# Expert stage of a cross-attention and mixture-of-experts kernel: raw w1 in two buffers, the high part of the gelu output by a second gelu, gathers ahead of both scatters, unused units not taken

## What is computed

```
x = x + attention(layernorm(x), ctx)            # 16 heads, 154 keys
n = layernorm(x)
for each expert e of 8:                         # two best of softmax(n @ router_w.T)
    h = gelu(n @ w1[e].T)                       # 256 -> 1024, exact gelu
    out = out + weight_e[:, None] * (h @ w2[e].T)   # 1024 -> 256
x = x + out
```

## Time and profile before

| | |
|---|---|
| median of 3 runs | 501.27 us |
| profiled execution | 504.29 us, its span 502.1 us |
| mean granted TensorE clock | 0.938 |
| PE busy | 430.2 us, 86% of the span |
| DVE busy | 364.7 us |
| POOL busy | 263.7 us |
| ACT busy | 222.6 us |
| expert stage (first matmul of `up(0)` to the end) | 237.44 to 502.1 us |

### The profile page before, as it was taken

How to read it: one execution, slowest core, us unless ns; L and a number is a source line. 1 busy time by engine, 2 the same in 40 slices (tenths; PEclk the granted TensorE clock), 3 DMA queues, 4 the chain that set the end, 5 groups by cost and what they waited for, 6 DMA issues and landing times.

```text
span 502.1 us, 11066 instructions
## 1 busy us (share of the span) xinstructions
PE 430.2 (86%) x3429; PEld 378.6 (75%) x3430; DVE 364.7 (73%) x789; ACT 222.6 (44%) x433; POOL 263.7 (53%) x308
## 2 busy tenths in 40 slices
PE   7678999999999998317489999999998699999960
PEld 3577888888888886213389989889997698989950
DVE  2678999999999996596576776765578848775520
ACT  1556667677666775130334424422355444423210
POOL 2678877777787776103304444445434444444452
PEclk9899999999999999657969999999999999999985
DMA  8401112111112111501452542722246734323232
GB/s 236 163 1 44 65 64 76 52 62 53 58 57 84 52 64 33 185 6 42 163 204 44 172 81 44 210 44 44 42 107 171 206 97 110 49 43 54 33 55 33
DMA packets 24769, 42.72 MB, mean 85 GB/s; under 512 B 6048, under 2 KB 19232, under 8 KB 22688
## 3 DMA queue, kind: packets, MB, share of 16 engines
q1 hardware_dynamic: 13664, 28.68, 16.8%
q0 software_dynamic: 7584, 10.80, 12.7%
q10 hardware_dynamic: 3488, 2.83, 1.8%
HBM read 26.54 MB, written 9.45 MB: 72 GB/s over the span
## 4 chain that ended last, share of the span: by engine, by line
PE 59%; DMA 13%; DVE 11%; issue 8%; POOL 5%; ACT 2%; ACTq 1%; DVEq 1%; POOLq 0%
PE ps_s L1245 12%; PE ps_s L1091 10%; PE ps_t L1262 10%; DMA result<-big,rowtok 6%; PE ps_t L1106 6%; PE ps_t L1265 5%; DMA big<-rows,gtok 4%; PE ps_a L1124 3%; PE ps_c L1141 3%; PE ps_a L1047 2%; DMA XS<-in_x 2%; PE ps_a L1119 2%; PE ps_c L1228 2%; PE ps_c L1153 1%; PE ps_c L1147 1%
## 5 line engine op out<-in xcount | busy, mean ns | idle before, releaser
L477 POOL DMA_INDIRECT result<-big,rowtok x38 | 65.3, 1717 | 123.8 <-DVE big L1018 59.7
L1245 PE MATMUL ps_s<-xgT,KB 128*128 128x256 f32 x912 | 113.1, 284 | 12.4 <-DVE KB L933 9.4
L1245 PEld LDWEIGHTS ps_s<-xgT,KB 128*128 128x128 f32 x912 | 110.7, 192 | 14.4 <-DVE KB L933 9.7
L1091 PE MATMUL ps_s<-KB 128*128 (+1 forms) x384 | 72.3, 325 | 9.4 <-DVE V_all L733 3.2
L618 ACT ACTIVATE big<-ps_s 128x512 f32<-128x512 f32 x76 | 44.8, 596 | 74.6 <-PE ps_s L1245 71.3
L446 POOL DMA_INDIRECT big<-rows,gtok x44 | 48.2, 1095 | 52.1 <-DVE gtok L949 24.0
L1091 PEld LDWEIGHTS ps_s<-KB 128*128 128x128 f32 x384 | 57.2, 194 | 14.3 <-issue 7.6
L626 ACT ACTIVATE big<-ps_t,wrow 128x256 f32<-128x256 f32 x38 | 18.0, 474 | 97.0 <-PE ps_t L1265 92.4
L1262 PE MATMUL ps_t<-KB,HTb 128*128 x160 | 57.8, 401 | 0.0
L553 ACT ACTIVATE PT<-ps_t 128x512 f32<-128x512 f32 x80 | 47.5, 599 | 21.5 <-PE ps_t L1106 19.7
L383 POOL TENSOR_TENSOR half<-big 128x256 f32<-128x256 f32 x64 | 47.4, 740 | 16.4 <-ACT big L545 16.1
(11 more groups left out here) (159 smaller groups left out, 779.2 us busy)
## 6 DMA issues: line engine op xcount, KB each, us to landing
big<-in_wexp SPq DMA_DIRECT2D x16, 1024.0 KB
V_cur<-V_all SPq DMA_DIRECT2D x16, 384.0 KB, 2.6
result<-x SPq DMA_DIRECT2D x16, 128.0 KB, 1.7
rows<-xn SPq DMA_DIRECT2D x16, 128.0 KB, 2.1
XS<-in_x ACTq DMA_DIRECT2D x1, 1536.0 KB, 11.4
big<-rows,gtok POOLq DMA_INDIRECT x44
result<-big,rowtok POOLq DMA_INDIRECT x38
big<-in_ctxT SPq DMA_DIRECT2D x1, 308.0 KB, 3.6
```

Source lines behind the costliest of these rows:

```text
L477: pool.indirect_dma_start(out, bass.IndirectOffsetOnAxis(rowtok[:, u, h:h + 1], 0), ys[:, 2 * (u % 2) + h, :], None, compute_op=ALU.add).t ...
L1091: last = mm(ps_s[q % 2][:, j, 0:2 * KEYS].rearrange("p (h k) -> p h k", h=2), a[:, u, g, :], rhs, start=k == 0, stop=k == 2)
L1245: last = mm(ps_s[j // 4][:, j // 2 % 2, (j % 2) * PAIR:(j % 2 + 1) * PAIR], w1[:, w, k, j * P:(j + 1) * P], xgT[:, u % 2, a, k, :], start= ...
```

## The change

- Raw w1 gets two buffers, in space that the attention stage no longer uses (V_all, V_cur and PT are put in one tile VP). SP loads w1[0], w2[0], w1[1] before the first expert is used, and later w1[e+1] right behind w2[e].
- The high part of the gelu output is written by ACT with a second gelu of the same PSUM block (fp32r output), ahead of the plain one. DVE's rounding copy L989 goes; only the subtraction stays (`turn` becomes `low_part`). ACT waits for `down(s-2)` before the gelus of s, where DVE did.
- At the start of the stage DVE's order becomes `take_rows(0)`, `take_rows(1)`, `split_w1(1)`, `low_part(0)`, `split_w2(0)`.
- POOL issues both gathers of unit s+3 ahead of both scatters of s.
- Gathers, `take_rows` and row transposes from unit 16 on are under the condition that their unit is used.

```diff
-        V_all = sb("V_all", [P, B, VW])
-        V_cur = sb("V_cur", [P, 2, VW])
+        VP = sb("VP", [P, (B + 2) * VW + 5 * 4 * P])
+        V_all = VP[:, 0:B * VW].rearrange("p (b v) -> p b v", b=B)
+        V_cur = VP[:, B * VW:(B + 2) * VW].rearrange("p (u v) -> p u v", u=2)
+        PT = VP[:, (B + 2) * VW:].rearrange("p (k a n) -> p k a n", k=5, a=4)
+        wraw1 = VP[:, 0:2 * W1].rearrange("p (e w) -> p e w", e=2)
...
             sp.wait_ge(fold_made, 5 * TILES)
+            sp.wait_ge(pv_psum, TILES)
+            sp.dma_start(wraw1[:, 0, :], wexp[0, :, 0:W1]).then_inc(w1_loaded, 16)
             for e in range(E):
...
                 if e:
-                    sp.wait_ge(w1_lo, NP1 * e)
-                sp.dma_start(wraw1, wexp[e, :, 0:W1]).then_inc(w1_loaded, 16)
-                if e:
                     sp.wait_ge(w2_lo, e)
                 sp.dma_start(wraw2, wexp[e, :, W1:WB]).then_inc(w2_loaded, 16)
+                if e + 1 < E:
+                    sp.wait_ge(w1_loaded, 16 * (e + 1))
+                    if e:
+                        sp.wait_ge(w1_lo, NP1 * e)
+                    sp.dma_start(wraw1[:, (e + 1) % 2, :], wexp[e + 1, :, 0:W1]).then_inc(w1_loaded, 16)
...
                 if has(3):
-                    left_by(s + 1)
+                    with if_used(pool, s + 3):
+                        left_by(s + 1)
+                        for h in range(2):
+                            gather((u + 3) % 4, h)
                 for h in range(2):
-                    if has(3):
-                        gather((u + 3) % 4, h)
                     wait_alone(ys_made, 2 * s + h + 1)
...
-            def gelu(s):
+            def gelu(s, u):
+
+                if not isinstance(s, int) or s >= 2:
+                    act.wait_ge(down_psum, 2 * (s - 1))
                 for b in range(4):
                     act.wait_ge(up_psum, 4 * s + b + 1)
                     if not isinstance(s, int) or s >= 1:
                         act.wait_ge(hidT_lo, 4 * s + b - 3)
+                    act.activation(hidT[u % 2][:, 0, 2 * b:2 * b + 2, :],
+                                   ps_s[b // 2][:, b % 2, :].rearrange("p (j n) -> p j n", j=2), ACT.Gelu)
                     act.activation(hid[:, b, :], ps_s[b // 2][:, b % 2, :], ACT.Gelu).then_inc(hid_made, 1)
...
-            def turn(s, u):
-
-                if not isinstance(s, int) or s >= 2:
-                    dve.wait_ge(down_psum, 2 * (s - 1))
+            def low_part(s, u):
+
                 for b in range(4):
                     js = slice(2 * b, 2 * b + 2)
-                    src = hid[:, b, :].rearrange("p (j n) -> p j n", j=2)
                     dve.wait_ge(hid_made, 4 * s + b + 1)
-                    dve.tensor_copy(hidT[u % 2][:, 0, js, :], src).then_inc(hidT_hi, 1)
-                    dve.wait_ge(hidT_hi, 4 * s + b + 1)
-                    dve.tensor_tensor(hidT[u % 2][:, 1, js, :], src, hidT[u % 2][:, 0, js, :].bitcast(fp32),
-                                      ALU.subtract).then_inc(hidT_lo, 1)
+                    dve.tensor_tensor(hidT[u % 2][:, 1, js, :], hid[:, b, :].rearrange("p (j n) -> p j n", j=2),
+                                      hidT[u % 2][:, 0, js, :].bitcast(fp32), ALU.subtract).then_inc(hidT_lo, 1)
             take_rows(0, 0, True)
-            take_rows(1, 1, True)
-            split_w2(0, 0)
             read_used(dve)
             to_split = dve.value_load(table(t_split, 0), min_val=0, max_val=E * E - 1)
-            turn(0, 0)
+            take_rows(1, 1, True)
             with dve.If(to_split > 0):
                 split_w1(to_split % E)
+            low_part(0, 0)
+            split_w2(0, 0)
...
                 if has(2):
-                    take_rows(s + 2, (u + 2) % 4, has(4))
+                    with if_used(dve, s + 2):
+                        take_rows(s + 2, (u + 2) % 4, has(4))
...
                 if has(2):
-                    row_transposes(s + 2, (u + 2) % 4)
+                    with if_used(pe, s + 2):
+                        row_transposes(s + 2, (u + 2) % 4)
                 down(s, u, e0)
```

More of the change, by code:

```diff
@@ L95, in xattn_moe_kernel @@
         KTr = KB[:, o3:o3 + 2 * GROUPS * B * KEYS].rearrange("p (s g n) -> p s g n", s=2, g=GROUPS)
-        wraw1, wraw2 = big[:, 0:W1], big[:, W1:WB]
+        wraw2 = big[:, W1:WB]
         pr = sb("pr", [P, 2, HEADS, 32])
-        PT = sb("PT", [P, 5, 4, P])
         half = sb("half", [P, 4, 64])
@@ L218, in xattn_moe_kernel @@
             ("xgT_psum", "xgT_made", "gtok_made", "wr1", "wrow_made"))
-        up_psum, hid_made, hidT_hi, hidT_lo, xgT_hi = (sem(n) for n in
-            ("up_psum", "hid_made", "hidT_hi", "hidT_lo", "xgT_hi"))
+        up_psum, hid_made, hidT_lo, xgT_hi = (sem(n) for n in
+            ("up_psum", "hid_made", "hidT_lo", "xgT_hi"))
         down_psum, low_made, ys_made, added = sem("down_psum"), sem("low_made"), sem("ys_made"), sem("added")
@@ L603, in split_w1 @@
                 for cols in PARTS1:
-                    act.activation(ws1[:, 0, cols], wraw1[:, cols], ACT.Copy).then_inc(w1_hi, 1)
+                    src = wraw1[:, e % 2, cols] if isinstance(e, int) else wraw1[:, bass.ds(e % 2, 1), cols].squeeze(1)
+                    act.activation(ws1[:, 0, cols], src, ACT.Copy).then_inc(w1_hi, 1)
             def split_w2(e, par):
@@ L635, in _ @@
             to_split = act.value_load(table(t_split, 0), min_val=0, max_val=E * E - 1)
-            gelu(0)
+            gelu(0, 0)
             with act.If(to_split > 0):
@@ L646, in pair @@
                     with if_used(act, s + 1):
-                        gelu(s + 1)
+                        gelu(s + 1, (u + 1) % 4)
                     with act.If(to_split % E > 0):
@@ L932, in split_w1 @@
                     dve.wait_ge(w1_hi, NP1 * e + n + 1)
-                    dve.tensor_tensor(ws1[:, 1, cols], wraw1[:, cols], ws1[:, 0, cols].bitcast(fp32),
+                    src = wraw1[:, e % 2, cols] if isinstance(e, int) else wraw1[:, bass.ds(e % 2, 1), cols].squeeze(1)
+                    dve.tensor_tensor(ws1[:, 1, cols], src, ws1[:, 0, cols].bitcast(fp32),
                                       ALU.subtract).then_inc(w1_lo, 1)
@@ L1008, in pair @@
                     with if_used(dve, s + 1):
-                        turn(s + 1, (u + 1) % 4)
+                        low_part(s + 1, (u + 1) % 4)
                     with dve.If(to_split % E > 0):
```

## The result

The kernel before took 502.02 us in the comparison (median of 4 runs, 500.98 to 503.67), the changed one 497.3 (494.24 to 503.44): ratio .987 [.983, .991]. It is faster, by about 6.5 us (1.3%) and not by 13.2, and lies outside the range of 484.5 to 493.5. Ratios leave out executions that fell in a slower state (here the one of 503.44 us); medians and ranges are of all executions. The profiled execution of that comparison was that longest of its four.

The account below looks back on a forecast made before the run. The prediction took PE as the bound in the middle of the stage. Start +0.9, middle -11.5 and end -2.6 summed to -13.2 us: span 488.9 from 502.1, or 488.1 us against the median of 501.27, range 484.5 to 493.5.

Parts of the forecast that it names:

- Start: Stage's start through `up(2)`: `up(1)` comes 6.3 us earlier, yet `up(2)` ends at 274.1 against 273.24, 0.9 us later.
- `up(2)` waits for these rows and starts at 266.5: Start: `up(2)` is held until `take_rows(2)` is done, so it starts only 1.1 us earlier than before.
- has 7.9 us to spare: Start: a short stop ahead of `up(1)` may lower the clock, but 258.6 has 7.9 us to spare.
- 2.0: Start: PE resumes at the low clock after standing still, which adds 2.0 us to `up(2)`, 2.8 at most.
- Middle: Transposes of unit 3 to those of unit 19: 12.1 us lost, 0.6 stays, gain 11.5, at the least 8.5.
- 12.1 of loss: Middle: 16 units take 198.5 us against 186.4 at 11.65 us a unit without a wait.
- Gathers go: Middle: both gathers issued 5 to 7 us earlier, so all seven gather waits go, 6.6 us, with their restarts.
- End: Last scatters: no gather between them (1.3), scatter(17, 0) earlier (0.4), a shorter landing (0.9): gain 2.6 us, 0.8 to 4.0.
- The middle pays only in part: Rival: start +5, middle 6 won, end 1, other waits replacing the gathers: 499 to 494 us, chance 0.10.
- The start pays as well: Rival: `up(2)` freed from the late w2[1] starts at 258.6 without the low clock: 478.2 us, chance 0.08.
- ACT becomes the bound: Rival: a gelu writing fp32r takes 1.92 us, so ACT delays the rows: 541 us, chance 0.03.

Follow-up runs that it names:

- c_layout: The kernel before with only V_all, V_cur and PT joined in one allocation ahead of `big`: 505.87 us, ratio 1.0046 against the kernel before.
- d_layout_last: The kernel before with V_all, V_cur and PT joined in one allocation placed behind `pr`: 505.71 us, ratio 1.006 against the kernel before.
- a_again: The changed kernel run again unedited, for a second profile: 496.03 us, ratio .9869 against the kernel before.
- b_gback: The changed kernel with the second gather of unit s+3 back between the two scatters of s: 523.8 us, ratio 1.031 against the kernel before.
- c_geluback: The changed kernel with the second gelu undone, DVE's rounding copy and its wait for `down(s-2)` back: 503.4 us, ratio .999 against the kernel before.
- b_uncond: The changed kernel with gathers, `take_rows` and row transposes of unused units back: 497.97 us, ratio .988 against the kernel before.
- a_w2first: The changed kernel with DVE's `split_w2(0)` moved ahead of `take_rows(1)`: 487.49 us, ratio .9683 against the kernel before.
- c_gback_apart: b_gback with SP issuing the load of w1[e+1] before it waits for w2's low part: 520.54 us, no ratio given.
- b_look2: The kernel before run again unedited, for a third profile: 503.18 us.
- f_gback_pieces: b_gback with DVE's 128x2048 instruction for w2's low part cut in four pieces: 509.1 us, ratio 1.013 against the kernel before.
- b_look1: The kernel before run again unedited, for a second profile: 501.56 us.

## Why the prediction was wrong

The sign and the mechanisms were right; the time was not, since four terms were mis-sized, three of them costs taken as nothing.

- **Ahead of `up(0)`** the sum had no term. The diff's first hunk, V, V_cur and PT in one allocation, was read as a matter of names. It costs 0.5% by itself in the kernel before (c_layout, d_layout_last), 2 to 3 us; 2.7 measured here, 1.9 over all profiles. No row of before could show it; of the four terms it is the one most off.
- **Start, +0.9 forecast, +2.4 measured.** "`up(2)` waits for these rows and starts at 266.5", 29.1 us after `up(0)`, holds where `up(0)` runs at the high clock, as it did in the earlier trace rows's execution: 29.24 us in the first profile of the changed kernel. In a_again it is 31.1 (30.7 to 31.1 in the four profiles of this start with a slow `up(0)`), since `up(0)` took 7.51 us, and ACT's part of w1[1], DVE's low parts, `split_w2(0)`, the load and the rows all follow from its end. The step that failed is the base, `up(0)` at the high clock: in the kernel before a slow `up(0)` costs nothing, in the changed one 1.8 us. The slow `up(1)` is absorbed, as "has 7.9 us to spare" said, and the "2.0" taken for the low clock in `up(2)` is 1.8 (7.38 less 5.6).
- **Middle, -11.5 forecast, -10.3 measured.** All seven gather waits are gone; one wait for rows of 0.25 us is left at unit 12 (0.3 forecast). The forecast's 12.1 of loss was read from the first profile (198.5 us); the other profiles have 197.9, which is 0.6 of the 1.2. The rest is the pace: (187.6 - 0.25) / 16 = 11.71 us a unit and not 11.65. "Gathers go" was right, its reason incomplete: their old place costs some 22 us in the changed kernel (b_gback), because changed timing puts more of them inside DVE's long instruction, and the stop of 4.1 us that the prediction read as a late issue alone shows the same pattern. The second gelu takes 0.60 us by itself; eight in a row start 0.48 apart, where the prediction took a pace of 0.53. It hides, as forecast, and ACT is busier by 36 us, not 45. The Trainium skill, "ScalarE: Activation LUTs", section on what ACT_TABLE_LOAD costs, gives 0.61 for a single one by its formula, and here the trace agrees with its 0.60. What the copy's move from DVE is worth had no number of its own in the prediction: c_geluback shows some 6 us, more of it at the start than in the middle. That is no step that failed, as the forecast's chain of the start already went without the copies.
- **End, -2.6 forecast, -1.3 measured.** The row of scatters is 4.0 shorter than in b_uncond; some 2.6 come back in POOL's DRAIN (3.63 to 6.28 us), which the sum took as a constant.
- **Rivals.** "The middle pays only in part", at 494 to 499 us and a chance of 0.10, gave the right time by luck, for the wrong reason: the middle paid 10.3 of 11.5. "The start pays as well" came true only by a_w2first's own edit, which frees w2[1]: 487.49 us, not 478.2, as the start's clock and the two terms above still stand against it. "ACT becomes the bound" fell: 0.60 us is half of the 1.2 from which it decides.
- **The range** does not follow from its own bounds: start, middle and end all at their worst give 501.27 + 3.5 - 8.5 - 0.8 = 495.5 us, all at their best 485.0. The text says that not all fall at one end, but only the upper end was drawn in, to 493.5, while the lower one lies at 484.5. It had no bound for what the change was thought not to touch, the stretch ahead of `up(0)` and the DRAIN.

## What to carry to other kernels

When a load waits for a step that frees its buffer, look first at the step's place on its engine: here moving one instruction, at no cost, was worth 8.5 us, and the second buffer for the neighbouring tensor nothing that could be measured. Before forecasting, give the untouched stages and the kernel's closing work a term with bounds, and take the base from more than one profile where the clock ahead of the change can be at either level. Where a load waits for a long instruction of DVE, keep gathers and scatters of POOL from starting within that instruction: issue them earlier, or cut it in pieces. And put nothing that is needed soon behind a scatter that goes out with such a load.

## What the runs showed of the hardware

- **POOL's indirect DMA is held by a long instruction of DVE.** Gathers take 0.99 us alone. Begun within DVE's 2.29 us instruction they take 0.83 to 0.90 us more than what was left of it: 2.99 with 2.12 left (b_gback), 3.10 with 2.24 (c_gback_apart), 2.22 with 1.39 (b_look2), 1.58 with 0.72 (the kernel before). A scatter, 1.6 alone, took 3.73 with 2.22 left (first profile of the changed kernel). A gather that started 0.02 us after DVE's instruction was not held (b_look2, 0.99). Cutting that instruction takes some 9 us off b_gback. The Trainium skill, "SBUF — State Buffer", section "SBUF: two separate sides", says that the two engines share a port pair that is locked for a whole instruction; by that rule the hold ends with DVE's instruction, and the traces agree. But there it is a DVE instruction in a two-port mode that keeps GpSimd from writing the descriptors of its DMAs; for one with two SBUF inputs, as this `tensor_tensor`, the section names a conflict only with a GpSimd instruction that reads SBUF, and section "Who interferes with whom" says that `tensor_tensor` did not stall a DMA. Here it did, and the measurement decides. Whether the gather's reading of its indices from SBUF is what conflicts, no run shows.
- **A gather or scatter whose packets come behind loads of 1 MB is late by them**: a gather lands 8.89 us after its start with two loads issued (b_gback), 7.72 with one (c_gback_apart), 2.81 ahead of the load (b_look2); a scatter 9.92 and 11.08 with two, 3.80 without (f_gback_pieces, first profile of the changed kernel).
- **POOL's closing DRAIN varies**: 3.63 to 3.67 us in the kernels with the unused gathers at the end, 6.28 without, 5.63 with six early unread ones. Its cause is open.
- **Joining allocations moves the landing of loads** at the kernel's start, and `up(0)` by 1.9 us in the mean. Its cause is open too.
- **`up(0)`, behind a wait of 1.5 us, ran at either clock** in executions of the same or nearly the same kernel: 5.9 us at a granted clock of 1.00 (first profile of the changed kernel) or 7.3 to 7.5 at 0.77 to 0.78 (a_again, b_look1).
